# Spectral layer: the mixing products in fp16 parts, split by ScalarE and GpSimd, and issued later in TensorE's order

## The chip, the cores and the metric

The kernel runs on one core of a Trainium2 chip. The metric is the device time of one launch in microseconds (us). Engines are named as in the profile: PE (TensorE, with PEld for its weight loads), DVE (VectorE), ACT (ScalarE), POOL (GpSimd), SP (SyncE, which only issues transfers).

## The reference

The program is a small model of four stages (a scan over an image with a convolution, a deformable convolution, two attentions with experts, and a spectral layer). The change concerns the last, the spectral layer. Of it the reference computes, for 4 images of 2304 tokens with 128 channels:

```
U_plus, U_minus = causal convolution of u (and of u with alternating signs) with 16 filters phi[:, k]
out  = einsum('btkd,k,kde->bte', U_plus,  sigma ** 0.25, M_phi_plus)
out += einsum('btkd,k,kde->bte', U_minus, sigma ** 0.25, M_phi_minus)
out += sum over i < 3 of  u delayed by i  @  M_u[i]
x = x + sum over 4 weights m of  weight[m] * out_m(first T / (1, 2, 4, 8) tokens)
```

The last line has four sets of matrices, each used on a shorter head of the tokens, weighted by a softmax that is made one-hot in value. The second index of each product, `kde`, is what this document calls the mixing: 128 channels of one filter's convolved sums times a 128x128 matrix.

## The kernel before, in words

Everything around the change is in `layer3_spectral`; one image after the other (`nc.Fori(0, NB)`), each with a preparing block and a main block. The preparing block splits the image's tokens into even and odd ones, turns them on PE and keeps them as fp16 high and low parts in `xt`. The main block loops over the 16 filters in pairs (`filters_pair(i, last)`), and each filter has 4 units (NU = 4): z chooses the even or odd taps of the filter, q the even or odd tokens. So there are 4 x 16 x 4 = 256 units in all, and a pair's 8 units are unrolled in the code.

A unit convolves 1152 tokens (three thirds of 384) with one half of a filter. The three thirds come from shared partial sums, so that PE writes five groups of fp16 products (128x128 weights, 128 columns each) into three PSUM banks OWN, PAIR and LOW: `shared` (9 products), `shared_pairs` (9), `first` (a triangle of 15), `second` (9 and 9), a second triangle with 9 more, and `pairs` (9): 84 in all. Each fp16 value is a high and a low part, of which three products are summed.

ACT copies partial results out of PSUM: `own_s`, `pair_s`, `low_s` and `pair_1`. DVE combines them to the three sums of 384 columns: the first in `low_s` (two additions), the second in `Uc[:, 0]` (three), the third in `Uc[:, 1]` (five, with `pair_2`). Then PE mixes each sum (`mix(u, c)`, c = 0 to 2) in fp32, with the fp32 matrices `Wm`, and accumulates into PSUM banks 0 to 4, where all filters of an image add up. `totals` cuts a sum by the four heads of tokens: pieces of 144, 144 and 96 columns, of 192 and 192, and of three times 128.

Engines run their instructions in the order written here and wait on semaphores: `s_cv` counts PE's finished groups (6 in a unit), `s_ea` ACT's copies (4), `s_ed` DVE's steps (12). DVE also makes the next filter's `Wm` between these steps (`mix_step`, spread over the units of a filter: two 512-wide additions, two scalings and six multiply-adds in four units). SP loads filters and matrices one filter ahead. POOL has no work in the main block.

Before this layer, `layer3_attention` runs a causal attention over each image; POOL has no work there either.

Of the kernel before, what the change touches and what calls it, by code (L numbers as in the profile page):

```python
# [1845 lines left out]
def layer3_attention(nc, w):  # L1846
    with ExitStack() as ctx:
# [13 lines left out]
        O = sb("O", [P, 2, C])  # L1861
        loads = [(wq[:], w["wq"]), (wk[:], w["wk"]), (wv[:], w["wv"]), (ones_c[:], w["ones_c"]),
# [5 lines left out]
        with nc.Block() as block:  # L1868
            @block.sync
            def _(sp):  # L1870
                for dst, src in loads:
                    sp.dma_start(dst, src).then_inc(s_w, 16)

            @block.gpsimd
            def _(pool):
                pool.wait_ge(s_w, 16 * len(loads))
# [4 lines left out]
        with nc.Fori(0, NB) as b:  # L1881
# [37 lines left out]
            with nc.Block() as block:  # L1919
                @block.tensor  # L1920
# [134 lines left out]
def layer3_spectral(nc, w, f_scr, f_sum, out):  # L2055
# [12 lines left out]
    with ExitStack() as ctx:  # L2068
# [21 lines left out]
        own_s, pair_s = sb("own_s", [P, 2, RC]), sb("pair_s", [P, 2, RC])  # L2090
        pair_1, pair_2 = sb("pair_1", [P, RC]), sb("pair_2", [P, RC])
# [14 lines left out]
        mscale = sb("mscale", [P, KF + 1, 2])  # L2106

# [6 lines left out]
        s_ed = sem("combined")  # L2114
        with nc.Block() as block:
# [12 lines left out]
            @block.gpsimd  # L2128
            def _(pool):
                pool.wait_ge(s_w, 16 * len(loads))  # L2130

            @block.tensor
            def _(pe):
                pe.wait_ge(s_tr, 1)
                pe.matmul(ps[:, 0:NF], top_rep[:], ident[0:NF, 0:NF], start=True, stop=True).then_inc(s_tp, 1)

            @block.vector
            def _(dve):
# [21 lines left out]
                st.link(dve.tensor_scalar(mu[:, 0], mu[:, 0], wt[:, 0:1], None, ALU.mult))  # L2160
                for m in range(1, 4):
                    st.link(dve.scalar_tensor_tensor(mu[:, m], mu[:, m], wt[:, m:m + 1], mu[:, m - 1], ALU.mult, ALU.add))

                dve.wait_ge(s_ta, 1)
# [3 lines left out]
                dve.tensor_scalar(top_rep[:], ones_c[0:NF, :], top[:, 0:1], 128.0 * 2.0 ** -23, ALU.mult, ALU.mult).then_inc(s_tr, 1)  # L2168
                st.link(dve.tensor_scalar(taps, taps, top_inv[:, 0:1], 2.0 ** 13, ALU.mult, ALU.mult))
# [15 lines left out]
                for at, n, of in ((0, 2, sums[:, :, P:P + SETW]), (2, 4, threes)):  # L2185
# [6 lines left out]
                                          sg[:].unsqueeze(2).broadcast_to([P, KF, 2]), ALU.mult))  # L2192
                for m in range(4):
                    dve.tensor_scalar(mweight[:, :, :, m:m + 1], mscale[:].unsqueeze(3), wt[:, m:m + 1], None, ALU.mult)

            @block.scalar
            def _(act):
# [6 lines left out]
                act.activation(taps_abs, taps, ACT.Abs).then_inc(s_ta, 1)  # L2204

        normalize(nc, ctx, sem, "st_ln", ps, xres, xn, ones_c[:], w["eps5"])

        s_xp, s_xc, s_xd, s_tt, s_tc, s_tl = (sem(n) for n in ("x_copied", "x_ordered", "x_differences", "turned", "first_part", "second_part"))
        XS = 2.0 ** 10
# [40 lines left out]
        with nc.Fori(0, NB) as b:  # L2250
# [61 lines left out]
            with nc.Block() as block:  # L2312
# [31 lines left out]
                def _(pe):  # L2344
# [51 lines left out]
                    def mix(u, c):  # L2396

                        r, z, q, _ = shape(u)
                        for m, lo, hi, o in totals(z ^ q, c):
                            src = low_s if c == 0 else Uc[:, c - 1]  # L2400
                            mm = pe.matmul(ps[:, o:o + hi - lo], Wm[:, r, z, m, :], src[:, lo - c * RC:hi - c * RC],  # L2401
                                           start=False, stop=False, skip_group_check=True)
                        return mm
# [14 lines left out]

                    pe.wait_ge(s_fl[0], (b * (KF // 2) + 1) * 64)
# [3 lines left out]
                    second(0, b * KF * NU * 4)  # L2423

                    def filters_pair(i, last):
                        unit = (b * KF + i * 2) * NU
                        for u in range(2 * NU):
                            r, q = u // NU, u % 2
# [11 lines left out]
                            pe.wait_ge(s_ed, done + 5)  # L2440
                            mix(u, 1)
                            v = (u + 1) % (2 * NU)
                            if not (last and v == 0):
# [8 lines left out]
                            pe.wait_ge(s_ed, done + 12)  # L2452
                            mm = mix(u, 2)
                            if u % NU == NU - 1:
                                mm.then_inc(s_kd[r], 1)
# [6 lines left out]
                def _(dve):  # L2462
# [29 lines left out]
                    with dve.Fori(0, KF // 2) as i:  # L2492
                        unit = (b * KF + i * 2) * NU
                        for u in range(2 * NU):
# [9 lines left out]
                            dve.tensor_tensor(second, ps[:, OWN:OWN + RC], pair_1[:], ALU.add).then_inc(s_ed, 1)  # L2504
# [3 lines left out]
                            if step < 5:  # L2508
                                mix_step(i * 2 + r + 1, i + r, 1 - r, step, base + (i * 2 + r + 1) * 8)
                            dve.wait_ge(s_cv, (unit + u) * 6 + 5)  # L2510
# [186 lines left out]
```

## Time and profile before

| | |
|---|---|
| Timed runs | 7707.59, 7712.57, 7712.93 us; median 7712.57 |
| Profiled execution: span from first to last instruction | 7975.8 us (no other time is given for it) |
| Granted TensorE clock, mean over the span | 0.955 |
| Main blocks of the spectral layer in the span | 6071 to 6517, 6553 to 6999, 7036 to 7481, 7519 to 7964 us |

The profiled execution took 263 us (3.4%) more than the median of the timed runs; a stage's time below is the profiled one. Engine busy times overlap, so they don't add up to the span. PE's busy time counts pipelined products, so the spacing of the groups' starts, not the duration of one product, tells what PE takes for them.

### The profile page before, as it was taken

What the parts mean: (1) busy time and instruction counts of PE and PEld (TensorE: products, weight loads), DVE (VectorE), ACT (ScalarE), POOL (GpSimd) and SP (SyncE); (2) the same over time, 40 slices, a digit from 0 to 9 for tenths busy, and PEclk for the clock granted to TensorE, in tenths of its full rate; (3) what the DMA queues carried; (4) which work ended last, traced back from release to release, by engine and by line L of the source; (5) the groups of instructions that cost most, each with busy time, mean ns of one, the idle gap of its engine ahead of it and who ended that gap; (6) DMA issues with size and microseconds to landing.
All of it is one profiled execution on the core that took longest, in us unless ns stands there. A gap on an engine that the chain in (4) does not pass through costs nothing. (4 is left out here: it accounts for less than half of the span.)

```text
span 7975.8 us, 170513 instructions
## 1 busy us (share of the span) xinstructions
PE 7187.8 (90%) x62522; PEld 6186.6 (78%) x62522; DVE 5972.5 (75%) x9085; ACT 4078.3 (51%) x8541; POOL 3659.8 (46%) x4037
## 2 busy tenths in 40 slices
PE   8999899998999989999756788879988999999999
PEld 6888778886788867888546666645667989989999
DVE  7999889997899978999644555545556767767677
ACT  5888668885688757888311222224543222222222
POOL 5888658885688847888355555410000000000000
PEclk9999999999999999999878899889998999999999
DMA  2333223332233322333366555400003434434343
GB/s 66 90 93 93 75 64 92 93 90 68 74 90 93 92 58 83 90 94 90 109 174 171 164 160 152 119 4 3 0 6 95 125 116 125 125 116 128 113 129 108
DMA packets 590364, 763.42 MB, mean 96 GB/s; under 512 B 51703, under 2 KB 527896, under 8 KB 587585
## 3 DMA queue, kind: packets, MB, share of 16 engines
q1 hardware_dynamic: 537921, 585.72, 25.8%
q0 software_dynamic: 51840, 169.91, 7.5%
q8 instruction: 348, 5.70, 0.3%
q14 instruction: 255, 2.09, 0.1%
HBM read 721.77 MB, written 33.66 MB: 95 GB/s over the span
## 5 line engine op out<-in xcount | busy, mean ns | idle before, releaser
L647 POOL TENSOR_TENSOR l_arena<-l_arena 128x768 f32<-128x768 f32 x1536 | 2591.3, 1688 | 449.1 <-DVE l_arena L579 443.6
L579 DVE TENSOR_TENSOR_SCAN l_arena<-l_arena,psum 128x772 f32<-128x772 f32 x1536 | 2664.5, 1751 | 176.6 <-PE psum L406 72.5
L500 ACT ACTIVATE l_arena<-l_arena,l_A 128x384 f32<-128x384 f32 x3072 | 1643.7, 604 | 38.2 <-DVE l_arena L579 32.7
L408 PE MATMUL psum<-l_arena 128*128 128x128 f32 x11520 | 1499.3, 280 | 46.8 <-DVE l_arena L579 43.0
L408 PEld LDWEIGHTS psum<-l_arena 128*128 128x128 f32 x11520 | 1367.4, 192 | 170.5 <-issue 146.7
L419 PE MATMUL psum<-l_ident,l_arena 128*128 128x128 f32 x9216 | 1257.6, 273 | 50.6 <-ACT l_yT L506 41.7
L419 PEld LDWEIGHTS psum<-l_ident,l_arena 128*128 128x128 f32 x9216 | 1055.2, 141 | 60.2 <-POOL l_arena L647 60.2
L2269 POOL TENSOR_TENSOR st_mab<-st_xr 128x384 f32<-128x384 f32 x8 | 7.8, 1000 | 2053.1 <-DVE st_xr L2259 2053.1
L1211 POOL DMA_INDIRECT l_G<-neighbours,l_idx x648 | 621.2, 959 | 650.2 <-PE psum L1259 301.0
L490 ACT ACTIVATE l_arena<-l_arena,l_BT 128x256 f32<-128x256 f32 x1728 | 747.0, 496 | 7.5
L2544 ACT ACTIVATE st_own_s<-psum 128x384 f32<-128x384 f32 x256 | 125.7, 491 | 1092.5 <-PE psum L2381 1092.5
L1259 PE MATMUL psum<-l_ident,l_G 128*128 128x128 f32 x2592 | 361.8, 301 | 181.2 <-ACT l_val L1384 109.8
L2381 PE MATMUL psum<-st_FS,st_xt 128*128 128x128 f16 x6912 | 518.0, 219 | 4.4 <-DMA st_FS<-filter_sums 4.4
L556 DVE TENSOR_TENSOR l_arena<-psum,l_BT 128x384 f32<-128x384 f32 x960 | 510.8, 532 | 0.0
L1259 PEld LDWEIGHTS psum<-l_ident,l_G 128*128 128x128 f32 x2592 | 333.5, 157 | 212.6 <-issue 198.4
L406 PEld LDWEIGHTS psum<-l_ident,l_arena 128*128 128x128 f32 x3456 | 380.5, 140 | 143.8 <-issue 141.3
L406 PE MATMUL psum<-l_ident,l_arena 128*128 128x128 f32 x3456 | 486.9, 277 | 2.8 <-DVE l_arena L579 2.8
L2401 PE MATMUL psum<-st_Uc,st_Wm 128*128 128x128 f32 (+1 forms) x2560 | 448.6, 306 | 6.4 <-DVE st_Uc L2521 6.4
L2381 PEld LDWEIGHTS psum<-st_FS,st_xt 128*128 128x128 f16 x6912 | 434.7, 97 | 21.1 <-DMA st_FS<-filter_sums 4.8
L1054 DVE TENSOR_TENSOR l_G<-l_G,psum 128x1536 f32<-128x1536 f32 (+1 forms) x144 | 365.5, 2547 | 84.2 <-DMA l_G<-neighbours,l_idx 73.9
L2371 PE MATMUL psum<-st_F,st_xt 128*128 128x128 f16 x4608 | 427.4, 219 | 0.0
L2401 PEld LDWEIGHTS psum<-st_Uc,st_Wm 128*128 128x128 f32 x2560 | 351.4, 191 | 7.5 <-DVE st_Uc L2521 7.5
(436 smaller groups left out, 11291.5 us busy)
## 6 DMA issues: line engine op xcount, KB each, us to landing
l_arena<-c_rows SPq DMA_DIRECT2D x1536, 192.0 KB, 3.1
st_FS<-filter_sums SPq DMA_DIRECT2D x128, 1155.0 KB, 9.2
st_F<-filter_parts SPq DMA_DIRECT2D x128, 320.5 KB, 7.2
neighbours<-l_xt SPq DMA_DIRECT2D x256, 72.0 KB
st_mab<-in_st_mp SPq DMA_DIRECT2D x68, 256.0 KB, 9.5
st_mab<-in_st_mm SPq DMA_DIRECT2D x68, 256.0 KB, 6.2
l_G<-neighbours,l_idx POOLq DMA_INDIRECT x648
l_arena<-in_x SPq DMA_DIRECT2D x4, 1152.0 KB, 5.2
```

The lines of the kernel that those rows point to most:

```text
L406: mm = pe.transpose(ps[:, o:o + P], xT[:, rank[s] % 2, t, h * P:(h + 1) * P], ident[:])
L408: mm = pe.matmul(ps[:, o:o + P], dtuT[:, g % 2, t, h * P:(h + 1) * P], diagB[:, rank[s] % 3, t, :], start=True, stop=True)
L419: mm = pe.matmul(y_ps[:, t, h * P:(h + 1) * P], hC[:, s % NHC, h, t * P:(t + 1) * P], ident[:], start=(n == 0 and h == 0 and t % 2 == 0), ...
L490: ins = act.activation(xT[:, i % 2, t, :], dtuT[:, g % 2, t, :], ACT.Copy, scale=BT[:, g % 2, t, n:n + 1])
L500: act.activation(decay[:, s % NDC, half(h)], dtv[:, g % 2, h, :], ACT.Exp, scale=A[:, g // NRC, h, n:n + 1]).then_inc(s_exp, 1)
L556: dve.tensor_tensor(diagB[:, i % 3], ident_ps.unsqueeze(1).broadcast_to([P, LB, P]), BT[:, g % 2, :, n:n + 1].broadcast_to([P, LB, P]), AL ...
L579: dve.tensor_tensor_scan(hbuf[:, n, run], decay[:, s % NDC, run], x2_ps[s % 2][:, run], 0.0, ALU.mult, ALU.add).then_inc(s_scan, 1)
L647: pool.tensor_tensor(hC[:, s % NHC], halves(hbuf[:, s % NS, :]), Cs[:, s % NCS, :].unsqueeze(1).broadcast_to([P, 2, RC]), ALU.mult).then_i ...
L1211: pool.indirect_dma_start(out=G[:, g, 4 * k:4 * k + 4, :].rearrange("p q c -> p (q c)"), out_offset=None, in_=tables[b], in_offset=bass.In ...
L1259: mm = pe.matmul(bank(i % 2, P * a, P * (a + 1)), G[:, g, 4 * k + q, :], ident[:], start=(q == 0), stop=(q == 3), is_transpose=True, skip_ ...
L2381: mm = pe.matmul(ps[:, at + i * P:at + (i + 1) * P], xt[:, xpart, x0 + LB - 1 - i, :], FS[:, r, fpart, z, three, shift + i * P:shift + (i ...
L2401: mm = pe.matmul(ps[:, o:o + hi - lo], Wm[:, r, z, m, :], src[:, lo - c * RC:hi - c * RC], start=False, stop=False, skip_group_check=True)
```

## The change

Each mixing is now made of fp16 products. ACT copies each of the three sums to fp16 (the high part, `U16[:, c, 0]`), POOL subtracts that from the fp32 sum and writes the rest as fp16 (the low part, `U16[:, c, 1]`). The matrices `Wm` are split in the same way into `W16`. A mixing is then three rounds over the same pieces: high sum by high matrix, high by low, low by high; 24 products of a unit in place of 8 in fp32 (an fp32 product stands as two instructions in the trace).

The order of PE's work in a unit changes too: the second triangle is made at the end of the unit before (`third`), mixing 0 comes after `pairs`, mixing 1 after the next unit's `shared` and `shared_pairs`, and mixing 2 after the next unit's `first`, `second` and `third`. ACT's four copies are reordered so that the next unit's three (`keep`) stand between the high parts of the second and third sum. DVE keeps its order, but for `mix_step`, whose first call moves behind the third sum's PSUM steps, and one wait more: it doesn't overwrite the third sum until the low part of the unit before is made.

So that fp16 holds the sums, the scale of the matrices changes: `layer3_attention` has new work for POOL, which loads all 16 pairs of matrices (four per image), squares and adds them up (1024 columns at a time, and a tree of ten additions at the end) to a bound, `peak`; the spectral layer's first block turns it into a factor (`grow`, and `shrink`, which the last additions to the stream multiply by). `own_s`, `pair_s`, `pair_1` and `pair_2` now lie in the buffer `xr`, to make room.

```diff
@@ layer3_attention, in each image's second block
+                    for j in range(NKB):
+                        own = tile[:, j % 2].rearrange("p i c -> p (i c)")
+                        pool.wait_ge(s_tl[j % 2], b * NKB * 16 + 32 * (j // 2 + 1))
+                        pool.tensor_tensor(own, own, own, ALU.mult).then_inc(s_pk, 1)
+                        pool.wait_ge(s_pk, base + 2 * j + 1)
+                        pool.tensor_tensor(power[:], power[:], own, ALU.add).then_inc(s_pk, 1)
...
@@ layer3_spectral, first block, DVE
+                dve.tensor_scalar(bound_rep, ones_c[:], w["peak"][:, 0:1], float(P), ALU.mult, ALU.mult).then_inc(s_bd, 1)
+
+                dve.wait_ge(s_bd, 2)
+                dve.tensor_reduce(bound[:, 0:1], ps[:, BANK:BANK + P], AX.X, ALU.max).then_inc(s_bd, 1)
...
+                dve.wait_ge(s_bd, 4)
+                st.link(dve.tensor_reduce(bound[:, 1:2], mscale[:].rearrange("p k z -> p (k z)"), AX.X, ALU.max))
...
@@ main block, PE
-                    def mix(u, c):
+                    def mix(i, u, c):
 
                         r, z, q, _ = shape(u)
-                        for m, lo, hi, o in totals(z ^ q, c):
-                            src = low_s if c == 0 else Uc[:, c - 1]
-                            mm = pe.matmul(ps[:, o:o + hi - lo], Wm[:, r, z, m, :], src[:, lo - c * RC:hi - c * RC],
-                                           start=False, stop=False, skip_group_check=True)
...
+                        for upart, wpart in ((0, 0), (0, 1), (1, 0)):
+                            if wpart == 0:
+                                pe.wait_ge((s_uh, s_ul)[upart], made + 3 * upart)
+                            for m, lo, hi, o in totals(z ^ q, c):
+                                mm = pe.matmul(ps[:, o:o + hi - lo], W16[:, r, wpart, z, m, :], U16[:, c, upart, lo - c * RC:hi - c * RC],
+                                               start=False, stop=False, skip_group_check=True)
...
-                            pe.wait_ge(s_ea, copied + 3)
-                            triangle(u, q * HB + 2 * LB, EDGE0 + q)
-                            own(u, LOW, 4, q * HB, False).then_inc(s_cv, 1)
-                            if u % NU == 0:
-                                pe.wait_ge(s_wm[r], use(i, r) + 1)
-                            pe.wait_ge(s_ed, done + 2)
-                            mix(u, 0)
...
                             pe.wait_ge(s_ea, copied + 4)
                             pairs(u, FS[:, :, :, :, 1], 0, True).then_inc(s_cv, 1)
...
-                            mix(u, 1)
+                            mix(i, u, 0)
+                            if more:
...
+                                pe.wait_ge(s_ed, done + 3)
                                 shared(v)
                                 pe.wait_ge(s_ed, done + 7)
                                 shared_pairs(v)
+                            mix(i, u, 1)
+                            if more:
                                 pe.wait_ge(s_ed, done + 9)
                                 first(v)
                                 second(v, copied + 4)
...
+                                third(v, copied + 4)
+                            mix(i, u, 2)
...
@@ main block, DVE
+                            dve.wait_ge(s_ul, (unit + u) * 3 + 3)
                             dve.tensor_tensor(third, low_ps[:, 0:RC], own_s[:, u % 2, :], ALU.subtract).then_inc(s_ed, 1)
...
@@ main block, ACT and POOL
+                    def high(unit, u, c, done):
+                        act.wait_ge(s_ed, (unit + u) * 12 + 24 + done)
+                        act.activation(U16[:, c, 0, :], low_s[:, 0:RC] if c == 0 else Uc[:, c - 1, :], ACT.Copy).then_inc(s_uh, 1)
+
+                    def mixing_high(i, r, z):
+                        act.wait_ge(s_wm[r], use(i, r) + 1)
+                        act.activation(W16[:, r, 0, z], Wm[:, r, z], ACT.Copy).then_inc(s_wh, 1)
...
+                            high(unit, u, 0, 2)
+                            high(unit, u, 1, 5)
...
+                                keep(unit, u + 1)
+                            high(unit, u, 2, 12)
...
+                    def low(unit, u, c):
+                        pool.wait_ge(s_uh, (unit + u) * 3 + c + 1)
+                        src = low_s[:, 0:RC] if c == 0 else Uc[:, c - 1, :]
+                        pool.tensor_tensor(U16[:, c, 1, :], src, U16[:, c, 0, :], ALU.subtract).then_inc(s_ul, 1)
+
+                    def mixing_low(made, r, z):
+                        pool.wait_ge(s_wh, made)
+                        pool.tensor_tensor(W16[:, r, 1, z], Wm[:, r, z], W16[:, r, 0, z], ALU.subtract).then_inc(s_wl[z][r], 1)
```

PE, the middle of one unit before: mixing 0 (low_s), `pairs`, mixing 1 (Uc), then the next unit's `shared` and `shared_pairs`. ISA and REGISTER_ALU rows are waits and the arithmetic for them.

```order
L2436 ISA
L2401 MATMUL psum<-st_low_s,st_Wm 128x144 x2
L2401 MATMUL psum<-st_low_s,st_Wm 128x96
L2438 REGISTER_ALU
L2391 MATMUL psum<-st_FS,st_xt 128x128 x9
L2440 REGISTER_ALU
L2401 MATMUL psum<-st_Uc,st_Wm 128x192 x2
L2445 ISA
L2381 MATMUL psum<-st_FS,st_xt 128x128 x9
L2447 REGISTER_ALU
L2391 MATMUL psum<-st_F,st_xt 128x128 x9
```

PE at the same place after the change: `pairs` (L2442), mixing 0 in its three rounds (L2457, with the waits for the high and for the low part at L2455), then the next unit's `shared` (L2432).

```order
L2496 ISA
L2442 MATMUL psum<-st_FS,st_xt 128x128 x9
L2455 ISA
L2457 MATMUL psum<-st_U,st_W 128x144 x2
L2457 MATMUL psum<-st_U,st_W 128x96
L2457 MATMUL psum<-st_U,st_W 128x144 x2
L2457 MATMUL psum<-st_U,st_W 128x96
L2455 REGISTER_ALU
L2457 MATMUL psum<-st_U,st_W 128x144 x2
L2457 MATMUL psum<-st_U,st_W 128x96
L2502 ISA
L2432 MATMUL psum<-st_FS,st_xt 128x128 x9
```

Mixing 0 now stands behind `pairs`, in three times as many products, and mixing 1 has left its place ahead of `shared`.

ACT, one unit before: `own_s`, `pair_s`, `low_s` and `pair_1`, each out of PSUM.

```order
L2541 ISA
L2543 ISA
L2544 ACTIVATE st_own_s<-psum 128x384
L2545 REGISTER_ALU
L2546 ACTIVATE st_pair_s<-psum 128x384
L2547 REGISTER_ALU
L2548 ACTIVATE st_low_s<-psum 128x512
L2549 REGISTER_ALU
L2551 REGISTER_ALU
L2552 ACTIVATE st_pair<-psum 128x384
```

ACT after the change, from just behind `pair_1`: two high parts (L2607), the next unit's `own_s` and `pair_s` (now in st_xr) and `low_s`, then the third high part.

```order
L2607 ACTIVATE st_U<-st_low_s 128x384
L2606 REGISTER_ALU
L2607 ACTIVATE st_U<-st_Uc 128x384
L2597 ISA
L2598 ISA
L2599 ACTIVATE st_xr<-psum 128x384
L2600 REGISTER_ALU
L2601 ACTIVATE st_xr<-psum 128x384
L2602 REGISTER_ALU
L2603 ACTIVATE st_low_s<-psum 128x512
L2606 REGISTER_ALU
L2607 ACTIVATE st_U<-st_Uc 128x384
```

Three copies are new in a unit, and the third sum's stands behind the next unit's three, which wait for PE.

POOL after the change, one unit in the second half of a filter and the start of the next (before, it has no row here): three low parts a unit (L2641), and a matrix part (L2645) after the second of them in the first and last unit of a filter.

```order
L2641 TENSOR_TENSOR st_U<-st_low_s,st_U 128x384
L2639 REGISTER_ALU
L2641 TENSOR_TENSOR st_U<-st_Uc,st_U 128x384
L2639 REGISTER_ALU
L2641 TENSOR_TENSOR st_U<-st_Uc,st_U 128x384
L2639 ISA
L2641 TENSOR_TENSOR st_U<-st_low_s,st_U 128x384
L2639 REGISTER_ALU
L2641 TENSOR_TENSOR st_U<-st_Uc,st_U 128x384
L2644 REGISTER_ALU
L2645 TENSOR_TENSOR st_W<-st_Wm,st_W 128x512
```

All of these rows are new work of POOL's, with two inputs in SBUF each.

## Rows read from the trace of the kernel before

**Rows 1.** Windows: third main block: length, PE, PEld, DVE, ACT, POOL busy, clock, DMA.

```profile
7036.00:7481.00 445.00, 443.10 (x6394) 437.82 (x6394) 325.07 (x925) 128.48 (x256) 0.00 (x0) 1.00 0.41 120
```

**Rows 2.** Timeline of one unit: start us, duration us, engine, line, operation [idle before].

```profile
7100.26 0.49 ACT L2544 ACTIVATE st_own_s<-psum 128x384 f32<-128x384 f32 x1 [4.07 <-PE psum L2381]
...
7101.34 0.67 PE L2381 MATMUL psum<-st_FS,st_xt 128*128 128x128 f16 x9
7101.54 0.60 ACT L2548 ACTIVATE st_low_s<-psum 128x512 f32<-128x512 f32 x1 [0.36 <-PE psum L2371]
7101.85 0.67 PE L2391 MATMUL psum<-st_FS,st_xt 128*128 128x128 f16 x9
...
7102.36 0.88 PE L2401 MATMUL psum<-st_Uc,st_Wm 128*128 128x128 f32 x6
...
7103.08 0.33 PE L2371 MATMUL psum<-st_F,st_xt 128*128 128x128 f16 x3
...
7104.44 0.90 PE L2401 MATMUL psum<-st_low_s,st_Wm 128*128 128x144 f32 x6
...
7105.18 0.67 PE L2391 MATMUL psum<-st_FS,st_xt 128*128 128x128 f16 x9
7105.69 0.87 PE L2401 MATMUL psum<-st_Uc,st_Wm 128*128 128x192 f32 x4
7105.89 0.56 DVE L2513 TENSOR_TENSOR st_pair<-psum,st_pair_s 128x384 f32<-128x384 f32 x1 [0.52 <-PE psum L2391]
7106.36 0.28 DVE L2515 TENSOR_TENSOR st_Uc<-st_Uc,psum 128x128 f32<-128x128 f32 x1
7106.39 0.68 PE L2381 MATMUL psum<-st_FS,st_xt 128*128 128x128 f16 x9
...
7107.19 0.49 ACT L2544 ACTIVATE st_own_s<-psum 128x384 f32<-128x384 f32 x1 [4.06 <-PE psum L2381]
```

**Rows 3.** Groups by line, DVE from 6500 us: count, busy us, mean ns, idle.

```profile
L2518 DVE TENSOR_TENSOR st_Uc<-st_Uc,st_pair 128x384 f32<-128x384 f32 x195 | 108.8, 558 | 6.8
...
L2482 DVE SCALAR_TENSOR_TENSOR st_Wm<-st_Wm,st_mweight 128x128 f32<-128x128 f32 x310 | 94.4, 346 | 0.3
L2520 DVE TENSOR_TENSOR st_Uc<-st_Uc,st_pair 128x256 f32<-128x256 f32 x195 | 82.9, 425 | 6.8
...
L2507 DVE TENSOR_TENSOR st_Uc<-st_Uc,st_pair 128x128 f32<-128x128 f32 x194 | 55.2, 285 | 0.0
...
L2470 DVE TENSOR_TENSOR st_Wm<-st_mab 128x512 f32<-128x512 f32 x51 | 34.9, 685 | 0.0
```

**Rows 4.** Groups by line, POOL, whole span, in the same columns.

```profile
L2273 POOL TENSOR_TENSOR st_mab<-st_xr 128x256 f32<-128x256 f32 x12 | 8.4, 727 | 0.0
L2269 POOL TENSOR_TENSOR st_mab<-st_xr 128x384 f32<-128x384 f32 x8 | 7.8, 1000 | 2053.1 <-DVE st_xr L2259 2053.1
```

**Rows 5.** Timeline of the experts' stage, POOL and DVE, columns as in rows 2.

```profile
5302.62 1.26 POOL L1802 TENSOR_TENSOR mo_ep<-mo_ep 128x512 f32<-128x512 f32 x1 [169.72 <-DVE mo_ep L1788]
...
5307.32 0.41 DVE L1794 TENSOR_TENSOR mo_ep<-mo_ep 128x256 f32<-128x256 f32 x1
5307.48 1.38 POOL L1802 TENSOR_TENSOR mo_ep<-mo_ep 128x512 f32<-128x512 f32 x1 [0.86 <-DVE mo_ep L1788]
...
5369.27 1.38 POOL L1802 TENSOR_TENSOR mo_ep<-mo_ep 128x512 f32<-128x512 f32 x1 [1.71 <-DVE mo_ep L1788]
5369.44 0.28 DVE L1780 TENSOR_TENSOR stream<-stream,psum 128x128 f32<-128x128 f32 x1
```

**Rows 6.** Groups by line, ACT from 6500 us, in the same columns as rows 3.

```profile
L2308 ACT ACTIVATE st_xt<-psum 128x384 f16<-128x384 f32 x42 | 18.2, 507 | 17.1 <-PE psum L2299 14.8
```

**Rows 7.** Attention, first 27 us of an image: window, then DVE's mask line.

```profile
5473.00:5500.00 27.00, 24.96 (x141) 17.46 (x141) 18.85 (x51) 18.15 (x44) 0.00 (x0) 1.00 0.00 1
...
L2012 DVE TENSOR_TENSOR ca_S<-ca_S,ca_mask 128x128 f32<-128x128 f32 x9 | 2.6, 285 | 15.2 <-ACT ca_S L1992 15.2
```

**Rows 8.** Timeline, the last mixing of the second image, columns as in rows 2.

```profile
6999.49 0.94 PE L2401 MATMUL psum<-st_Uc,st_Wm 128*128 128x128 f32 x6 [1.59 <-DVE st_Uc L2521]
```

More of the change, by code:

```diff
@@ L1861, in layer3_attention @@
         O = sb("O", [P, 2, C])
+        tile = sb("tile", [P, 2, 2, 4 * C])
+        power = sb("power", [P, 2 * 4 * C])
+        s_tl, s_pk = [sem(f"matrices_loaded_{r}") for r in range(2)], sem("power_step")
+        NKB = KF // NB
+        TREE = 10
         loads = [(wq[:], w["wq"]), (wk[:], w["wk"]), (wv[:], w["wv"]), (ones_c[:], w["ones_c"]),
@@ L2114, in layer3_spectral @@
         s_ed = sem("combined")
+        s_uh, s_ul, s_wh = (sem(n) for n in ("outputs_high", "outputs_low", "mixing_high"))
+        s_wl = [[sem(f"mixing_low_{z}_{r}") for r in range(2)] for z in range(2)]
+        s_bd = sem("bound_spread")
         with nc.Block() as block:
@@ L2423, in _ @@
                     second(0, b * KF * NU * 4)
+                    third(0, b * KF * NU * 4)
                     def filters_pair(i, last):
@@ L2503, in _ @@
                             dve.wait_ge(s_ea, (unit + u) * 4 + 4)
-                            dve.tensor_tensor(second, ps[:, OWN:OWN + RC], pair_1[:], ALU.add).then_inc(s_ed, 1)
+                            dve.tensor_tensor(second, ps[:, OWN:OWN + RC], pair_1, ALU.add).then_inc(s_ed, 1)
                             dve.wait_ge(s_ed, at + 3)
@@ L2516, in _ @@
                             dve.tensor_tensor(third[:, 2 * P:], third[:, 2 * P:], low_ps[:, RC:], ALU.subtract).then_inc(s_ed, 1)
+                            if step < 5:
+                                mix_step(i * 2 + r + 1, i + r, 1 - r, step, base + (i * 2 + r + 1) * 8)
                             dve.wait_ge(s_ed, at + 9)
-                            dve.tensor_tensor(third, third, pair_2[:], ALU.add).then_inc(s_ed, 1)
+                            dve.tensor_tensor(third, third, pair_2, ALU.add).then_inc(s_ed, 1)
                             dve.wait_ge(s_ed, at + 10)
@@ L2533, in _, with keep @@
                                 xs = xs.rearrange("p (o x) -> p o x", o=2)
-                            dve.tensor_tensor(xs, xs, src, ALU.add).then_inc(s_res, 1)
+                            dve.scalar_tensor_tensor(xs, src, shrink[:, 0:1], xs, ALU.mult, ALU.add).then_inc(s_res, 1)
                 @block.scalar
                 def _(act):
-                    with act.Fori(0, KF // 2) as i:
+                    def keep(unit, u):
+                        act.wait_ge(s_cv, (unit + u) * 6 + 1)
+                        act.wait_ge(s_ed, (unit + u) * 12 + 9)
+                        act.activation(own_s[:, u % 2, :], ps[:, OWN:OWN + RC], ACT.Copy).then_inc(s_ea, 1)
+                        act.wait_ge(s_cv, (unit + u) * 6 + 2)
+                        act.activation(pair_s[:, u % 2, :], ps[:, PAIR:PAIR + RC], ACT.Copy).then_inc(s_ea, 1)
+                        act.wait_ge(s_cv, (unit + u) * 6 + 3)
+                        act.activation(low_s[:], ps[:, LOW:LOW + BANK], ACT.Copy).then_inc(s_ea, 1)
@@ L2547, in _ @@
-                            act.wait_ge(s_cv, (unit + u) * 6 + 3)
-                            act.activation(low_s[:], ps[:, LOW:LOW + BANK], ACT.Copy).then_inc(s_ea, 1)
+                            r = u // NU
                             act.wait_ge(s_cv, (unit + u) * 6 + 4)
                             act.wait_ge(s_ed, (unit + u) * 12 + 17)
-                            act.activation(pair_1[:], ps[:, PAIR:PAIR + RC], ACT.Copy).then_inc(s_ea, 1)
+                            act.activation(pair_1, ps[:, PAIR:PAIR + RC], ACT.Copy).then_inc(s_ea, 1)
@@ new lines, in filters_pair @@
+                            high(unit, u, 0, 2)
+                            high(unit, u, 1, 5)
+                            if u % NU == 0:
+                                mixing_high(i, r, 1)
+                            if u % NU == NU - 1:
+                                mixing_high(i + r, 1 - r, 0)
+                            if not (last and u == 2 * NU - 1):
+                                keep(unit, u + 1)
+                            high(unit, u, 2, 12)
+                    mixing_high(0, 0, 0)
@@ new lines, in _ @@
+                    keep(b * KF * NU, 0)
+                    with act.Fori(0, KF // 2 - 1) as i:
+                        filters_pair(i, False)
+                    filters_pair(KF // 2 - 1, True)
+                @block.gpsimd
+                def _(pool):
+                    def low(unit, u, c):
[5 more added lines that the diff above has]
+                        pool.tensor_tensor(W16[:, r, 1, z], Wm[:, r, z], W16[:, r, 0, z], ALU.subtract).then_inc(s_wl[z][r], 1)
+                    each = 2 * KF + 1
+                    mixing_low(b * each + 1, 0, 0)
+                    with pool.Fori(0, KF // 2) as i:
+                        unit = (b * KF + i * 2) * NU
+                        for u in range(2 * NU):
+                            r = u // NU
+                            low(unit, u, 0)
+                            low(unit, u, 1)
+                            if u % NU == 0:
+                                mixing_low(b * each + (i * 2 + r) * 2 + 2, r, 1)
+                            if u % NU == NU - 1:
+                                mixing_low(b * each + (i * 2 + r) * 2 + 3, 1 - r, 0)
+                            low(unit, u, 2)
```

83 lines of the change are left out of this document (55 added, 28 removed).

## Prediction

> **What bounds the kernel now.** I read the windows first, because only the four main blocks of the spectral layer change much. In the third of them PE is busy for 443.10 of 445.00 us at full clock, DVE for 325, ACT for 128, POOL for nothing [rows 1]; the other three read alike. So a main block lasts as long as PE's products, and every other engine has room. The timeline of one unit shows how tight that is. ACT's `own_s` starts at 7100.26 and in the next unit at 7107.19, so a unit takes 6.93 us. A group of nine fp16 products starts .51 us after the one before (7101.34, 7101.85, 7102.36), which is .0567 us a product. The three fp32 mixings fill 7102.36 to 7103.08 (.72), 7104.44 to 7105.18 (.74) and 7105.69 to 7106.39 (.70), together 2.16 us [rows 2]. The sum 84 x .0567 + 2.16 = 6.92 gives the unit: PE never stands still. The reader should keep two things from these rows. What PE saves in a mixing is saved in full as long as PE stays the bound; and DVE, with 325 of 445 us, has about 1.9 us of slack in a unit.
>
> **The cost of PE's part.** A mixing takes 1152 columns over the three sums; three fp16 rounds are 3456 columns, that is 27 times 128, and 27 x .0567 = 1.53 us. Pieces of 96, 144 and 192 columns in fp16 have no row. I scale them from the 128-column row, except that a 96-column piece may take no less than a 128-column one, which adds .04. The unit on PE alone is then 4.76 + 1.57 = 6.33 us. The gain is .60 us a unit, 154 us over 256 units. The lower bound of this gain (every piece as long as the 128-column spacing or its own share, whichever is more) is already in it, so PE's side has little doubt.
>
> **What is added for ACT and POOL.** ACT: three copies of 384 columns to fp16 a unit. The nearest rows are .49 (384 columns, fp32 out) [rows 2], .507 (384 columns, fp16 out of PSUM) [rows 6] and .60 (512 columns) [rows 2]; I take .51 and keep .49 and .60. With two 512-wide matrix copies in four units ACT goes from 128/64 = 2.0 [rows 1] to about 3.8 us of a 6.3 us unit, so its sum is no bound. POOL: three subtractions of 384 columns a unit. The fp32 row is 1.00, the 256-column row .727 [rows 4]; 128 columns cost .273 and the rest, .18, is fixed, so a 512-wide one is an estimated 1.27. No row has an fp16 operand on POOL; I take 1.00, with .73 and 1.27 as ends. With the matrix parts POOL has 3.0 + 1.27/2 = 3.64 us in a unit. That fits too, if POOL and DVE don't hinder each other.
>
> **Do they?** In the experts' stage POOL adds two SBUF operands (L1802) while DVE may be adding two SBUF operands too (L1794). Alone, POOL takes 1.26 us. With L1794 running until 5307.73 and POOL starting at 5307.48, it takes 1.38 [rows 5]. Of that overlap of .25 POOL's fixed part covers .14 to .18, so the extra .12 is the whole rest and not a share of it: POOL waits until DVE is through. An operation of DVE with one operand in PSUM (L1780) started inside such an addition adds nothing to the 1.38. So I expect operations with two SBUF inputs to exclude each other. What DVE does when POOL came first, no row shows: the ends are 0 and the whole of POOL's operation, 1.0. I take the whole, because the row shows waiting and not sharing.
>
> The Trainium skill's page "SBUF — State Buffer", section "Who interferes with whom", speaks against this change in the same way: a VectorE instruction with two SBUF inputs and a GpSimd one that reads SBUF hold a shared port one after the other, and whichever is second waits in full. The trace agrees for POOL as the second (.12 us), and nothing in it shows DVE as the second. By the page alone the unit would be 7.1 us or more; by the row alone, with POOL the only one to wait, 6.33.
>
> In a unit DVE has seven such operations, .558 + 2 x .425 + 4 x .285 = 2.55 us, and for the matrices (2 x .685 + 6 x .346)/4 = .86 [rows 3]. With POOL's 3.64 this is 7.05 us that can't overlap, against 6.33 on PE. Not all of an operation is exclusive (the fixed parts are not), so this is an upper figure, and the loop through a unit decides:
>
> - PE: the next unit's `shared_pairs`, mixing 1 and `first`: .51 + .51 + 15 x .0567 = 1.87 [rows 2].
> - PE to ACT .20 (7101.34 to 7101.54) [rows 2]; then ACT in its new order: `low_s` .60, the third sum's high part .51, `pair_1` .49, the low sums' high part .51: 2.11.
> - To POOL an estimated .10; the low part 1.00, and .30 for DVE's .425 operation that has just begun.
> - DVE: the second sum's last step, held until POOL is through, .285, then .555 and .555 for the third sum and `pair_2`, less two overlaps of .09 (7106.36 against 7105.89 + .56) [rows 2]: 1.22. To PE .06; `shared_pairs` waits for `pair_2`.
>
> Together 1.87 + .20 + 2.11 + .10 + 1.30 + 1.22 + .06 = 6.86 us. In the first unit of each filter the two 512-wide additions (1.37 us) stand ahead of the third sum's end; ACT's high part of that sum, and `pair_1` behind it, come about 1.0 later, .25 a unit on average. So the unit is 7.11 us: longer than 6.33 by .78, which eats the gain, and longer than 6.93 by .18, or 46 us over 256 units. What is late next is PE's `shared_pairs` (by some .45 a unit) and the low round of mixing 2, behind ACT and POOL.
>
> **The rest.** At an image's end nothing covers the last mixing. PE waits there 1.59 us for DVE's last step now [rows 8]; a copy and a subtraction come behind it, .51 + 1.00 + .20 = 1.7 us, 7 us in four images. The first block gets some ten small steps on DVE's own chain; none is wider than the mask's 128 columns at .285 [rows 7], so 3 us at most, which I take. The 32 last additions take a factor as well; a multiply-add of 128 columns takes .346 where an addition takes .285 [rows 3], 2 us in all, which stay within the margin of the 3. In the attention POOL's new work is 8 operations of 1024 columns an image, 2.36 each by [rows 4], and a tree of some 4: 23 us, within the first 27 us of a block, and the block goes on long after them. There DVE's mask addition (two SBUF inputs) occurs nine times [rows 7]. If each waits half a POOL operation, 11 us an image; DVE has 8 of the 27 us idle, PE 2. I take 3 an image, 12 in all, with 0 and 43 as ends. The matrices' extra transfers land while SP and the queues have nothing else (a DMA share of .00) [rows 7].
>
> Sum: 46 + 7 + 3 + 12 = 68 us. The rows come from an execution of 7975.8 us, 263 above the median of the timed runs; PE is at full clock in the main blocks, so I carry differences over unchanged: 7712.6 + 68 = 7780 us.
>
> **Rivals.**
>
> 1. **DVE doesn't wait for POOL** (faster). The loop loses the 1.00 of POOL and is under 5.9 us, so PE sets the unit at 6.33: -154 + 7 + 3 = -144, 7570 us. For it: no row shows DVE waiting. Against it: the waiting is complete where it is seen [rows 5]. It decides once the loop is under 6.78 us (6.93 less the 22 us of the rest and 15 us of margin, over 256).
> 2. **They exclude each other only while they stream.** Without fixed parts POOL's step is .82, its wait .15 and DVE's later start overlaps: the loop falls by some .35 with the matrix part, to 6.75 to 6.9, and the rest takes it back: 7690 to 7725, no change that can be measured. For it: the .14 to .18 that POOL's start doesn't share [rows 5].
> 3. **POOL is slower with fp16 beside fp32.** At 1.27 to 1.4 a subtraction, POOL's sum is 4.5 to 5 us and the shared time over 8; the loop grows by .3 to .4 and the waits of mixing 2 with it, to some 7.5: 256 x .57 + 22 = 168, 7880 us. Nothing in the rows speaks for or against it.
>
> **The numbers.** Forecast as above .45 (its own range 7735 to 7850), rival 1 .30, rival 2 .14, rival 3 .11. A change under .2% (15 us) can't be told from none here. Faster: rival 1 and the low edge of 2, .32; same: most of 2 and the low edge of the forecast, .13; slower .55. Rival 1 has more than 2 in 10, so the range takes it in: 7560 to 7860 leaves out most of rival 3 and the far ends.
>
> **What would show it.** If I am right, DVE's second step of `Uc[:, 0]` with 128 columns goes from 285 ns to about a microsecond while POOL's operations start before it, PE has a wait of some .4 us before `shared_pairs` in nearly every unit, and `own_s` recurs every 7.1 us. The two-SBUF operations of DVE at their old lengths beside POOL, and a PE without gaps, would prove rival 1; POOL rows of 1.3 us or more with no DVE operation beside them, rival 3. I am wrong above all if DVE's wait is not the whole of POOL's operation. A stretch of the main blocks with a granted clock under 1.00 would be something that I haven't costed.

## The result, and the profile after

The changed kernel takes 7843.24 us (median of 4 runs, 7841.85 to 7849.38) where the kernel before takes 7712.75 beside it: ratio 1.0176, 95% interval 1.0161 to 1.019, 130.5 us slower by the medians. The direction and the range of the prediction hold; its 68 us are about half of what was measured, and the runs show that forecast and measurement agree in sign for different reasons. The profiled execution has a span of 7839.8 us. The span of before stood 263 us higher than its runs, in the deformable convolution's stage (some 1125 us for 865), which the change doesn't touch, so I compare stages and not spans.

The windows of the changed kernel: its third main block, then the stretch around one jump back of TensorE's loop (length, PE, PEld, DVE, ACT, POOL busy, clock, DMA).

```profile
6841.00:7320.00 479.00, 430.67 (x6933) 413.73 (x6931) 389.75 (x936) 233.81 (x480) 220.64 (x224) 0.97 0.38 114
...
6904.00:6911.70 7.70, 2.81 (x44) 2.64 (x44) 3.89 (x11) 1.78 (x4) 2.02 (x2) 0.96 0.93 269
6911.70:6914.80 3.10, 3.02 (x31) 3.02 (x32) 0.49 (x2) 1.01 (x2) 0.33 (x1) 0.54 1.11 339
6914.80:6916.00 1.20, 1.20 (x25) 1.20 (x23) 0.36 (x1) 0.88 (x2) 0.58 (x1) 1.00 0.95 345
```

Against [rows 1] the block has become longer, yet PE is busy for 12 us less. It lost more by standing still: 48 of 479 us, where it was 2 of 445. Where, the waits of the changed kernel say (engine, line, what it waited for: us in all, times, longest).

```profile
PE psum L2442 <- issue: 75.0, 24, 3.5
PE psum L2422 <- issue: 38.0, 23, 4.0
...
PE psum L2457 <- POOL st_U L2641: 23.1, 48, 0.5
...
PEld psum L2442 <- DVE st_xr L2569: 75.4, 226, 0.7
```

The last row is the wait ahead of `shared_pairs` that I had forecast: 226 times, .33 us each. The first two rows I had not costed at all: 113 us in which PE waits for nothing that the profile shows, 24 and 23 times at the two lines. 24 is 6 jumps back of the loop over pairs of filters in each of 4 images. The timeline of PE at one of them:

```profile
6902.26 0.67 PE L2457 MATMUL psum<-st_U,st_W 128*128 128x128 f16 x9
6906.32 0.68 PE L2442 MATMUL psum<-st_FS,st_xt 128*128 128x128 f16 x9 [3.39 <-issue]
...
6908.86 0.28 PE L2422 MATMUL psum<-st_F,st_xt 128*128 128x128 f16 x2
6911.78 0.29 PE L2422 MATMUL psum<-st_F,st_xt 128*128 128x128 f16 x1 [2.65 <-issue]
6911.86 0.84 PE L2422 MATMUL psum<-st_FS,st_xt 128*128 128x128 f16 x6
6912.50 0.85 PE L2422 MATMUL psum<-st_F,st_xt 128*128 128x128 f16 x6
```

Mixing 2 of the last unit ends, the loop jumps back, and the first products of the body come 3.39 us late; 2.65 us are lost again a little on. Behind the second gap six products take .64 us (6911.86 to 6912.50), .107 each where .0567 is usual: the window above shows a clock of .54 for 3.1 us, the lower level of 1.2 GHz for nearly all of it, after PE had been busy for 2.81 of 7.70 us. The queue that carries instructions has grown (packets, MB, share of the engines' time), in the kernel before:

```profile
q8 instruction: 348, 5.70, 0.3%
```

and in the changed kernel:

```profile
q8 instruction: 570, 9.34, 0.5%
```

That is 16 KB a packet. PE's loop body had 84 x 8 fp16 products and 8 x 8 fp32 products of two passes, 800, each with a weight load, and 69 other instructions that the trace records: 1669. It has (84 + 24) x 8 = 864 with their loads, and 102 others, 1830 now.

VectorE and GpSimd in the unit without matrix work, in the timeline of the changed kernel:

```profile
7068.52 0.52 ACT L2607 ACTIVATE st_U<-st_low_s 128x384 f16<-128x384 f32 x1
...
7068.65 0.56 DVE L2561 TENSOR_TENSOR st_Uc<-psum,st_xr 128x384 f32<-128x384 f32 x1 [0.50 <-ACT st_xr L2619]
...
7069.11 0.92 POOL L2641 TENSOR_TENSOR st_U<-st_low_s,st_U 128x384 f16<-128x384 f32 x1
...
7069.24 1.06 DVE L2563 TENSOR_TENSOR st_Uc<-st_Uc,st_xr 128x256 f32<-128x256 f32 x1
...
7070.23 0.28 DVE L2564 TENSOR_TENSOR st_Uc<-st_Uc,st_xr 128x128 f32<-128x128 f32 x1
```

and the groups by line, in the columns of [rows 3]:

```profile
L2563 DVE TENSOR_TENSOR st_Uc<-st_Uc,st_xr 128x256 f32<-128x256 f32 x256 | 275.4, 1076 | 8.9
L2578 DVE TENSOR_TENSOR st_Uc<-st_Uc,st_xr 128x256 f32<-128x256 f32 x256 | 162.5, 635 | 8.8
L2561 DVE TENSOR_TENSOR st_Uc<-psum,st_xr 128x384 f32<-128x384 f32 x256 | 142.7, 557 | 120.4 <-ACT st_xr L2619 120.4
L2564 DVE TENSOR_TENSOR st_Uc<-st_Uc,st_xr 128x128 f32<-128x128 f32 x256 | 71.3, 278 | 0.0
...
L2641 POOL TENSOR_TENSOR st_U<-st_low_s,st_U 128x384 f16<-128x384 f32 x256 | 233.9, 914 | 66.6 <-ACT st_U L2607 50.8
```

POOL starts .13 us ahead of DVE's subtraction of 256 columns and ends at 7070.03; DVE's ends at 7070.30. So .425 [rows 3] has become 1.06, as a wait until POOL is through and .27 behind it. L2578, the same step of the third sum, is held in the 64 units in which GpSimd makes a matrix part beside it (1.27 us, and .42 in the others). The operation with an operand in PSUM (L2561) keeps the length that it had in the kernel before (group by line, from 6500 us):

```profile
L2504 DVE TENSOR_TENSOR st_Uc<-psum,st_pair 128x384 f32<-128x384 f32 x194 | 108.3, 558 | 96.4 <-ACT st_pair L2552 96.4
```

### The profile page after: what moved, and what is told of

It is laid out like the page before. It is cut to its first block and busy times, and to the rows that moved or that the text cites. A ratio compares the mean times of both kernels' runs of the same rounds, so it can differ in the third digit from the quotient of the medians.

```text
span 7839.8 us, 179804 instructions
## 1 busy us (share of the span) xinstructions
PE 7046.8 (90%) x64572; PEld 6018.8 (77%) x64572; DVE 6238.0 (80%) x9093; ACT 4510.7 (58%) x9442; POOL 4630.3 (59%) x5010
## 5 line engine op out<-in xcount | busy, mean ns | idle before, releaser
L2641 POOL TENSOR_TENSOR st_U<-st_Uc,st_U 128x384 f16<-128x384 f32 x512 | 469.3, 917 | 970.7 <-ACT st_U L2607 970.7
L2457 PE MATMUL psum<-st_U,st_W 128*128 128x128 f16 (+3 forms) x6144 | 532.0, 229 | 32.5 <-POOL st_U L2641 23.1
L2432 PE MATMUL psum<-st_FS,st_xt 128*128 128x128 f16 x6912 | 530.0, 222 | 0.4 <-DMA st_FS<-filter_sums 0.4
L2607 ACT ACTIVATE st_U<-st_Uc 128x384 f16<-128x384 f32 x512 | 266.2, 520 | 446.6 <-DVE st_Uc L2564 390.1
L2457 PEld LDWEIGHTS psum<-st_U,st_W 128*128 128x128 f16 x6144 | 413.2, 99 | 50.2 <-POOL st_U L2641 31.8
L2432 PEld LDWEIGHTS psum<-st_FS,st_xt 128*128 128x128 f16 x6912 | 431.6, 99 | 0.7 <-DMA st_FS<-filter_sums 0.6
L2442 PE MATMUL psum<-st_FS,st_xt 128*128 128x128 f16 x4608 | 351.1, 221 | 75.0 <-issue 75.0
L1259 PE MATMUL psum<-l_ident,l_G 128*128 128x128 f32 x2592 | 315.2, 281 | 71.1 <-DVE l_G L1054 43.0
```

The costliest lines, as they stand in the source:

```text
L2432: mm = pe.matmul(ps[:, at + i * P:at + (i + 1) * P], xt[:, xpart, x0 + LB - 1 - i, :], FS[:, r, fpart, z, three, shift + i * P:shift + (i ...
L2457: mm = pe.matmul(ps[:, o:o + hi - lo], W16[:, r, wpart, z, m, :], U16[:, c, upart, lo - c * RC:hi - c * RC], start=False, stop=False, skip ...
L2641: pool.tensor_tensor(U16[:, c, 1, :], src, U16[:, c, 0, :], ALU.subtract).then_inc(s_ul, 1)
```

## The experiments

Two theories. **F**: the loss is the code of PE's loop, which has grown past what stays resident and is fetched anew after each jump back. **L**: the loss is VectorE and GpSimd excluding each other (the lock), and the unnamed waits are part of it. The kernel before, timed again beside every round, came out between 7707.7 and 7712.75 us, so a difference between runs of different rounds is sure to some 5 us.

**1. TensorE's loop written out.** Nothing else is changed.

```diff
-with pe.Fori(0, KF // 2 - 1) as i:
-    filters_pair(i, False)
-filters_pair(KF // 2 - 1, True)
+for i in range(KF // 2):
+    filters_pair(i, i == KF // 2 - 1)
```

> The changed kernel with TensorE's loop over pairs of filters written out (no jump back within an image), the same products in the same order; the code of the layer on TensorE becomes about eight times as long. Theory F (code fetch): the 113 us that TensorE waits with 'issue' as the cause, 24 times at each of two lines, are the refetching of a loop body that has grown past what stays resident, and it shows at the jump back only; straight code is fetched ahead. So the waits at the second and third unit of a pair of filters go and the time falls by 113 to 133 us, to 7710 to 7730 us, although more code is fetched in all. Theory L (lock): these gaps are waits for low parts or for copies that the trace can't name, and the loss is VectorE's and GpSimd's; then the time stays within 10 us of 7843.

Measured: 7715.68 us, ratio to before 1.0008 (.9998 to 1.0017); 127.6 us less than the changed kernel. The waits with "issue" at these lines are gone; the groups of PE for the two lines (last column: idle before):

```profile
L2422 PE MATMUL psum<-st_F,st_xt 128*128 128x128 f16 x4608 | 427.2, 219 | 0.0
L2442 PE MATMUL psum<-st_FS,st_xt 128*128 128x128 f16 x4608 | 343.6, 219 | 0.0
```

and the instruction queue still carries

```profile
q8 instruction: 523, 8.57, 0.5%
```

So much the same amount of code is fetched, without a wait: it is the jump that costs, not the fetching. L says no change, and falls for this part of the loss.

**2, 3, 4. The kernel before with idle instructions.** 20, 8 and 4 ahead of each unit, a body of some 1828, 1732 and 1700 instructions.

```diff
 for u in range(2 * NU):
+    for n in range(20):   # 8, 4
+        pe.nop(hint="pad", nofuse=True)
```

> The kernel before with 20 idle instructions ahead of each unit on TensorE (160 in the loop body), nothing else. They bring the body from about 1668 instructions to about 1828, that of the changed kernel being about 1830; no GpSimd work, no low parts. Theory F: fetches of code in the main blocks rise from 63 to about 280 packets, 'issue' waits appear after each of the 24 jumps back, and the time grows by 80 to 130 us, to 7790 to 7845. Theory L: at most what 160 idle instructions cost in passing, under 20 us, to 7730 at most.

> The kernel before with 8 idle instructions ahead of each unit, not 20: a loop body of about 1732 instructions. What idle instructions cost in passing, by the run with 20: units away from the jump back took about 7.2 us for 6.93, so 8 cost some 0.1 us, 20 to 30 us in all. Theory F with a size above which the body is fetched anew: if 1732 still stays resident, 63 packets of code in the main blocks, no 'issue' waits at the jump, 7730 to 7740; if not, about 285 packets and the whole loss of some 130 us at once, 7840 to 7870. A loss that grows with each instruction (8/20 of 202 us, 81 us) would give 7790 and no such step.

> The kernel before with 4 idle instructions ahead of each unit: a body of about 1700 instructions, between 1668 (resident) and 1732 (fetched anew). Either 63 packets and 7705 to 7720, or about 280 and 7820 to 7840; a time between would mean that only a part of the body is fetched anew.

Measured: 7911.5 us (1.0266, 1.0249 to 1.0283), 7831.98 (1.0153, 1.0139 to 1.0168) and 7704.89 (.9996, .9985 to 1.0006). With 20 the loss is more than expected, because idle instructions cost some .2 to .3 us a unit in passing; with 8 they cost nothing there, units away from the jump take 6.90 to 6.95 as before, and 120 us come all at once. The waits and the timeline of PE with 8 idle instructions:

```profile
PE psum L2371 <- issue: 83.7, 28, 3.9
```

```profile
6372.13 0.88 PE L2401 MATMUL psum<-st_Uc,st_Wm 128*128 128x128 f32 x6
6376.25 0.50 PE L2371 MATMUL psum<-st_F,st_xt 128*128 128x128 f16 x3 [3.24 <-issue]
6376.55 0.84 PE L2371 MATMUL psum<-st_FS,st_xt 128*128 128x128 f16 x6
6377.19 0.85 PE L2371 MATMUL psum<-st_F,st_xt 128*128 128x128 f16 x6
```

It is the same picture, without GpSimd and without a new product: a gap, then products at .107. With 4 idle instructions nothing of it is there. The queue has, with 8 and then with 4:

```profile
q8 instruction: 566, 9.27, 0.5%
```

```profile
q8 instruction: 350, 5.73, 0.3%
```

There is a step between 1700 and 1732 instructions, and no slope: F.

**5. The kernel before, written out.** The edit of the first experiment.

> The kernel before with TensorE's loop over pairs of filters written out, a control: its body of about 1668 instructions isn't fetched anew now (63 packets of code in the main blocks, no 'issue' wait at the jump), so there is no stall to remove. Theory F: packets rise to about 240, as in the changed kernel written out, and the time stays, 7700 to 7720: straight code is fetched without a wait, and writing out is worth nothing where the body stays resident. If writing out has a gain of its own (loop registers, branches), it is faster by 15 us or more, and part of the 128 us of the first run isn't fetching.

Measured: 7705.27 us, .9997 (.9988 to 1.0007), with

```profile
q8 instruction: 504, 8.26, 0.4%
```

Writing out is worth nothing by itself; the 127.6 us were the stalls.

**6, 7. GpSimd without the low parts of the sums,** with TensorE's loop kept and with it written out. GpSimd waits and signals; the low parts are zeros, so one of the three rounds adds nothing to the result.

```diff
-src = low_s[:, 0:RC] if c == 0 else Uc[:, c - 1, :]
-pool.tensor_tensor(U16[:, c, 1, :], src, U16[:, c, 0, :], ALU.subtract).then_inc(s_ul, 1)
+pool.sem_inc(s_ul, 1)
...
+for c in range(3):
+    pool.memset(U16[:, c, 1, :], 0.0)
```

> The changed kernel, in which GpSimd doesn't make the low parts of the sums: it waits and signals as before, and the low parts are zeros written once an image, so this part of the result is left out. TensorE, ScalarE and VectorE have all their instructions. Theory F with a lock beside it: VectorE's subtraction of 256 columns falls from 1076 ns back to about 425, TensorE's wait ahead of the pair products (75 us) and its wait for low parts (23 to 32 us) go, the 113 us of 'issue' waits stay: 7843 less 75 to 110 is 7735 to 7770. Theory L alone (all of the loss is the lock): the 'issue' waits go as well and the time falls to 7600 to 7650.

> Both edits at once: TensorE's loop written out, and GpSimd doesn't make the low parts of the sums (zeros in their place; this part of the result is left out). If code fetch and the lock are two separate losses, the edits add: 7740 less the 128 us that writing out gave is 7612, with 7605 to 7630 allowed, since TensorE's products then follow one another with few waits. If the two hide behind one another (the gaps of the one are used by the other): 7640 or more.

Measured: 7740.18 us with the loop kept (1.0038, 1.0024 to 1.0052), 103 less than the changed kernel, and 7575.55 written out (.9823, .9809 to .9837), 140 less than the first experiment and below all that I expected. With the loop kept, VectorE's subtraction is back at its length of before, and the unnamed waits stay (groups, then waits):

```profile
L2563 DVE TENSOR_TENSOR st_Uc<-st_Uc,st_xr 128x256 f32<-128x256 f32 x256 | 108.8, 425 | 8.9
```

```profile
PE psum L2442 <- issue: 64.8, 25, 3.0
PE psum L2422 <- issue: 51.4, 24, 3.4
```

So the code of the loop and GpSimd's low parts are two losses. The 103 us are not the lock alone: without the low parts TensorE's wait for them (23.1 us in the changed kernel) is gone too, and no run divides the two. The losses don't add: apart they give 128 + 103 = 231 us, together 7843.24 - 7575.55 = 268. Some 37 us come free only when both are gone. I had expected losses that lie behind one another to show as less than the sum, which was wrong reasoning: it is more.

**8, 9. ScalarE's high part of the first sums ahead of its copy `pair_1`,** with the loop kept and written out.

```diff
+high(unit, u, 0, 2)
 act.wait_ge(s_cv, (unit + u) * 6 + 4)
 act.wait_ge(s_ed, (unit + u) * 12 + 17)
 act.activation(pair_1, ps[:, PAIR:PAIR + RC], ACT.Copy).then_inc(s_ea, 1)
-high(unit, u, 0, 2)
```

> The changed kernel with two of ScalarE's steps exchanged: the high part of the first sums is made before the copy of the first pair sums, so that GpSimd's low part runs half a microsecond earlier, beside VectorE's addition that reads PSUM and not beside its subtraction from two SBUF tiles. If the lock costs what TensorE's wait ahead of the pair products shows (75 us): the subtraction falls from 1076 ns to 450 to 650, and the time falls by 30 to 75 us, to 7770 to 7815. If the late copy of the pair sums holds VectorE up by as much: within 15 us of 7843. Theory F says nothing of this edit; the 'issue' waits stay.

> The changed kernel with TensorE's loop written out, and ScalarE's high part of the first sums ahead of its copy of the pair sums. If the two gains add: 7716 less 18 is 7698, 7685 to 7705, a little below the kernel before. If VectorE's slower subtraction was hidden once the stalls are gone: 7710 to 7720.

Measured: 7825.28 us (1.015, 1.0133 to 1.0167), and 7692.51 written out (.9982, .9971 to .9993). The subtraction falls to 463 ns, as expected:

```profile
L2563 DVE TENSOR_TENSOR st_Uc<-st_Uc,st_xr 128x256 f32<-128x256 f32 x256 | 118.5, 463 | 8.9
```

but 18 us is less than the 30 that I had as the least: of the .6 us that VectorE saves, it spends most waiting for the later `pair_1` (251.1 us ahead of L2561, for 120.4). Written out the gain adds as expected, 23 us, and this version is a little faster than the kernel before.

**10. VectorE's matrix steps spread over the units,** on top of 9: sum and difference of the matrices in two places, the four later steps one place on.

```diff
-                            dve.tensor_tensor(Wm[:, r, 1], mab[:, r, 0], mab[:, r, 1], ALU.subtract).then_inc(s_ad[r], 1)
                             return
+                        if step == 1:
+                            dve.tensor_tensor(Wm[:, r, 1], mab[:, r, 0], mab[:, r, 1], ALU.subtract).then_inc(s_ad[r], 1)
+                            return
-                        m = step - 1
+                        m = step - 2
...
```

> The run before this one, and VectorE's sum and difference of the matrices (0.85 and 1.64 us, in one place of every fourth unit, ahead of the last sums) in two places, with the later steps one place on. If VectorE's load in that unit sets the 7.40 and 6.83 us of the third and fourth unit of each filter, where others take 6.5: up to 0.95 us a filter of 64, so 15 to 50 us less than the run before, 7650 to 7685. If these units wait for GpSimd's low part of the matrices: no gain, within 8 us of the run before.

Measured: 7723.76 us (1.0015, 1.0007 to 1.0024), 31 slower than 9: a miss. The waits of PE show what I had overlooked:

```profile
PE psum L2442 <- ACT st_xr L2621: 47.4, 64, 0.7
```

The difference now stands at a unit's end, so the next unit's low sums come late; since 9, ScalarE waits for them ahead of `pair_1`, and PE for `pair_1`.

**11. The second matrix part one unit later,** on top of 9, so that GpSimd's 512 columns don't stand beside VectorE's difference of the matrices.

```diff
-                            if u % NU == 0:
+                            if u % NU == 1:
                                 mixing_high(i, r, 1)
...
-                            if u % NU == 0:
+                            if u % NU == 1:
                                 mixing_low(b * each + (i * 2 + r) * 2 + 2, r, 1)
```

> The version of 7692 us (TensorE's loop written out, high part of the first sums first), and the high and low part of each filter's second matrices one unit later, so that GpSimd's 1.5 us for them don't stand beside VectorE's difference of the matrices (1.59 us there, 1.14 where GpSimd is quiet). If the lock in that unit sets its 7.27 us: .45 us a filter, 29 us, less what the low part now costs beside the unit after: 7665 to 7685. If TensorE's wait there is for the low part of the last sums, which stand behind the matrices on VectorE: within 8 us of 7692.

Measured: 7679.29 us (.9962, .9949 to .9976), the fastest with the whole computation. In 9 and in 11, VectorE's difference:

```profile
L2526 DVE TENSOR_TENSOR st_Wm<-st_mab 128x512 f32<-128x512 f32 x68 | 107.9, 1587 | 0.0
```

```profile
L2526 DVE TENSOR_TENSOR st_Wm<-st_mab 128x512 f32<-128x512 f32 x68 | 46.1, 679 | 0.0
```

It is back at the .685 of [rows 3]; of the .9 us a filter, 58 in all, 13 come through to the end.

## Why the prediction came out as it did

**PE's products: right.** I had 6.33 us a unit for PE alone and a PE that saves .60. In experiment 7 `own_s` recurs every 6.29 us (6265.64 to 6661.93 for the second image's 63 units), and the time is 7575.55, with GpSimd's low parts left out, where I had 7570 for a PE that never waits. ScalarE's copies (.51 to .52 us in the timeline, .51 forecast) were right as well.

**VectorE waits for the whole of GpSimd's operation: right.** This was the open question, and rival 1, that it doesn't wait, is refuted by 1076 ns beside 425 in experiment 6. The Trainium skill, page "SBUF — State Buffer", section "Who interferes with whom", states this wait of the second comer for both engines; the trace agrees for VectorE as the second, by .13 us, and for operands in PSUM nothing is seen, L2561 at 557. Rival 2, that they exclude each other only while they stream, I had at .14, and part of it comes out: VectorE's 425 ns operation ends .27 us after GpSimd's, so .15 of it still overlaps, and the unit and time of this rival (6.75 to 6.9 us, 7690 to 7725) are those of the first experiment (6.82, 7715.68). So without the code the result would have been rival 2's and not the forecast's; though GpSimd waits for nothing where the rival gave it .15. Rival 3 is refuted: POOL takes 914 ns, less than the fp32 row, not more.

**The loop through a unit: wrong in its path and size.** I had 6.86 us and .25 for the matrices, 7.11 in all, with POOL delayed by .30 behind DVE's .425 operation and DVE's 128-column step held after it. In fact POOL comes first by .13 us. It waits for nothing, the 256-column step is the one that is held, and the 128-column step stays at 278 ns. With a POOL operation of .91 for 1.00 the loop is shorter: in the first experiment, where no jump disturbs it, the two shorter of every four units take 6.53 and 6.57 (the latter 6429.99 to 6436.56), and the second image's 63 units from 6300.54 to 6730.43 make 6.82 each, matrices included. So the term "46 us over 256 units" should have been (6.82 - 6.92) x 256, some -26. The change does save a little of the unit.

**What the sum lacked, and the step that failed: the code of PE's loop.** The prediction took it that a mixing in three rounds costs PE its columns and nothing else ("PE's side has little doubt"), so the longer loop stood at nothing. In the changed kernel the same 63 units go from 6328.58 to 6792.66, 7.37 each; .54 more than written out, 34 us in this image. The other three take 7.30 to 7.32 a unit where written out they take 6.82, so it is 127 us in all, 5.3 a jump. Measured by removal it is 127.6 us: the 113 us of unnamed waits, and the products at the lower clock behind them; together these would be more than 127.6, and that VectorE makes a part of it good meanwhile was not tried. The view that carried the warning was the order of instructions on PE, which showed mixings of three times as many products inside a loop; I counted their columns and not the instructions. The clock under 1.00 that I had named as a sign of something not costed is this: .97 for the block, .54 behind the gaps.

**The rest.** Attention: an image's cycle there grew from 128.5 to 131.4 us, 11 us for 12 forecast. Setup: .2 us for 3. Image ends: from the last `own_s` to the last mixing 11.1 us for 8.84, 9 in all for 7; but some 3 us more an image at the start of the next, 10 in all, had no term, and no run here divides them.

Written out, then, my terms as measured are -26, some 20, 11 and 0, 5 us in all, and the first experiment shows 7715.68 against 7709.03. The forecast of 68 was 63 too high in the terms that it had and lacked one of 128; that it lay in between is no merit.

## What to carry to other kernels

When a change adds instructions to a hardware loop, count the loop's instructions per engine before and after, weight loads included, and look whether the instruction queue carries more packets: here 32 more on TensorE, from some 1700 to some 1732, cost some 120 us by themselves. A loop that is too long is mended by a longer program: written out, much the same amount of code is fetched without a wait (experiment 1). An operation of GpSimd with SBUF inputs is best started where VectorE reads PSUM or waits, and what is put ahead of a copy that TensorE needs must not itself be late.

## What the runs showed of the hardware

- A loop body of some 1700 instructions on TensorE stays resident (350 packets, where the kernel before has 348) and one of some 1732 is fetched anew at each jump back (566 packets), at about 5 us a jump (120 to 128 us for 24). The Trainium skill, page "Runtime: NRT & Kernel Launch", section "Instruction fetch mechanics", states that a taken branch to code outside the fetched window stalls until it is fetched, and advises unrolling; the runs agree. It gives 2048 instructions for TensorE, and the step here lies lower. Whether the gap is that long because the loads of filters and matrices fill the queues in it (a DMA share of .93 in the window) wasn't tried, nor whether the step moves with the place of the body in the 16 KB packets.
- Straight code of about eight times the length is fetched without a wait that the profile shows (504 and 523 packets).
- A GpSimd subtraction from fp32 to fp16 of 384 columns takes 913 to 918 ns where the fp32 row had 1000 [rows 4].
